# Sixteen-wide attentions: q and k in two float32r parts, two heads in the two row halves of the array, all masks on TensorE

## What is computed

```python
# L0_attn_a
q = (x @ Wq.T).reshape(b, s, 16, 16); k, v likewise
scores = einsum('bqhd,bkhd->bhqk', q, k) / sqrt(16)
scores = where(causal, scores, min)
out = einsum('bhqk,bkhd->bqhd', softmax(scores), v).reshape(b, s, 256)
y = out @ Wo.T
# L0_ffn: gate_pre = h @ W_in.T + 0.1 * tanh(attention(x) @ A) * (h @ A) @ B
# L3_attn_a: the same attention with biases on q, k, v and the output
```

## Time and profile before

| | us |
|---|---|
| median of 3 runs | 2940.77 (2939.55 to 2943.56) |
| the profiled execution | 2940.94, of it span 2939.2 |
| PE busy | 2789.6 (95%), 16121 matmul records |
| DVE busy | 1611.8 (55%) |
| ACT busy | 1325.1 (45%) |
| POOL busy | 613.7 (21%) |

### The profile page before, as it was taken

The page is one execution under the profiler, slowest core; times in us unless marked ns, Lnnn a source line. Parts: engine busy times, 40 slices in busy tenths (PEclk is TensorE's granted clock), DMA queues, the critical chain, the costliest instruction groups (busy, mean ns, idle before and its releaser), DMA issues. The chain is left out here.

```text
span 2939.2 us, 44166 instructions
## 1 busy us (share of the span) xinstructions
PE 2789.6 (95%) x16121; PEld 1865.1 (63%) x16121; DVE 1611.8 (55%) x3495; ACT 1325.1 (45%) x2711; POOL 613.7 (21%) x737
## 2 busy tenths in 40 slices
PE   7989998999999998999999999999999999989979
PEld 4454475644676886887666666676676767754545
DVE  7758545677446766764333333454333332478587
ACT  3745634546443333334433433444343433336576
POOL 2021002030012331432000000023333331130185
PEclk9999999999999999999999999999999999999989
DMA  3021010030103421531000000010000000121031
GB/s 99 22 62 55 3 50 28 1 85 6 53 12 90 126 82 39 151 111 50 11 17 11 12 11 24 1 34 17 11 17 11 17 35 13 40 55 35 13 98 55
DMA packets 69377, 122.17 MB, mean 42 GB/s; under 512 B 15790, under 2 KB 44816, under 8 KB 68896
## 3 DMA queue, kind: packets, MB, share of 16 engines
q1 hardware_dynamic: 67564, 118.04, 13.5%
q10 hardware_dynamic: 1600, 1.31, 0.3%
HBM read 92.21 MB, written 1.54 MB: 32 GB/s over the span
## 5 line engine op out<-in xcount | busy, mean ns | idle before, releaser
L236 POOL TENSOR_TENSOR scale<-scale,powers 128x1 f32<-128x1 f32 (+1 forms) x98 | 57.4, 586 | 1370.4 <-DVE scale L217 1370.4
L130 PE MATMUL psum<-L1f_hT_part,L1f_wide 128*128 128x512 f32 x1104 | 270.8, 395 | 8.4 <-DVE L1f_inner L2566 5.9
L130 PEld LDWEIGHTS psum<-L1f_hT_part,L1f_wide 128*128 128x128 f32 x1104 | 202.6, 189 | 53.0 <-DVE L1f_inner L2566 10.4
L1702 ACT ACTIVATE L2b_tanh<-psum,L2b_inverse 128x512 f32<-128x512 f32 x192 | 110.6, 579 | 269.7 <-PE psum L1650 268.3
L1281 ACT ACTIVATE L0f_weights<-psum 128x512 f32<-128x512 f32 (+2 forms) x320 | 157.0, 566 | 95.3 <-PE psum L1097 75.1
L2374 POOL TENSOR_TENSOR L1f_inner<-L1f_inner,L1f_weight 128x512 f32<-128x512 f32 x96 | 144.3, 1510 | 265.4 <-DVE L1f_inner L2566 179.7
L2139 ACT ACTIVATE L2a_probs<-psum,L2a_negmax 128x512 f32<-128x512 f32 (+7 forms) x128 | 95.0, 742 | 172.3 <-DVE L2a_negmax L2173 172.2
L1659 PEld LDWEIGHTS psum<-L2b_v,L2b_weights 128*128 128x128 f32 x1152 | 141.3, 193 | 40.2 <-issue 28.7
L130 PE MATMUL psum<-L1f_down,L1f_inner_part 128*128 128x256 f32 x1152 | 153.1, 284 | 8.3 <-DVE L1f_down L2577 4.2
L130 PEld LDWEIGHTS psum<-L1f_down,L1f_inner_part 128*128 128x128 f32 x1152 | 148.9, 191 | 15.6 <-DVE L1f_inner_part L2582 9.9
L2183 DVE COPY L2a_probsT<-psum 128x512 f32<-128x512 f32 (+1 forms) x64 | 31.4, 491 | 228.0 <-PE psum L2039 228.0
(11 more groups left out here) (555 smaller groups left out, 6267.4 us busy)
## 6 DMA issues: line engine op xcount, KB each, us to landing
L1f_w<-in_L1f_w SPq DMA_DIRECT2D x32, 384.0 KB, 3.5
L1f_weight<-combine SPq DMA_DIRECT2D x32, 384.0 KB, 4.3
L1f_weight<-combine SPq DMA_DIRECT2D x32, 256.0 KB, 4.8
scan_spread_b<-bc SPq DMA_DIRECT2D x16, 512.0 KB, 3.7
L0f_qs<-L0f_part SPq DMA_DIRECT2D x96, 64.0 KB, 2.6
experts_early<-in_L1f_w SPq DMA_DIRECT2D x16, 384.0 KB, 4.3
L2a_early<-in_L2a_w SPq DMA_DIRECT2D x16, 384.0 KB, 2.9
L2b_early<-in_L2b_w SPq DMA_DIRECT2D x16, 384.0 KB, 3.0
```

The lines of the kernel that those rows point to most:

```text
L130: last = nc.tensor.matmul(to, stationary, moving, start=start and n == 0, stop=stop and n == len(pairs) - 1, skip_group_check=skip)
L1702: nc.scalar.activation(tanhs[u % 3][:, at:], ps_scores[u % 3][:, at:], ACT.Tanh, scale=inverse[e][:, NT + kt:NT + kt + 1]).then_inc(capped, 1)
```

## The change

`TERMS` falls to three products and the parts are float32r, two of them: the first part is written as float32r by ACT for all eight projections, the second is what is left, by one DVE instruction for each (POOL has none of it any more). A stack has 48 rows, with the two parts of the maximum 50. The four heads of a quad lie in pairs: heads 0 and 1 in partitions 0 to 49, heads 2 and 3 in partitions 64 to 113, so `quad_columns` orders the weights' columns anew. A matmul over rows 0 to 47 (or 49) is followed at once by one over rows 64 to 111 (or 113), into another PSUM bank. Pieces come in pairs (`two_pieces`), and a score slot is one pair of heads. The custom DVE instruction and `core.late` are gone: all pieces on the diagonal get their mask on PE, over 128 rows, right behind their pair. Piece 0 of a half is now two pieces of two heads. Each stack of a quad and half still takes 12 DMAs, of 32 partitions of float32 where there were 64 of bfloat16; the rows of the maximum take two DMAs where there was one, and so do the ones.

```diff
-TERMS = [(0, 0), (0, 1), (1, 0), (1, 1), (0, 2), (2, 0)]
+TERMS = [(0, 0), (0, 1), (1, 0)]
 SPLIT = HD * len(TERMS)
-WITH_MAX = SPLIT + 3
-STACKED = 16 * 2 * len(TERMS)
+WITH_MAX = SPLIT + 2
+STACKED = 16 * 2 * 2 * len(TERMS)
+BY_HALF = (0, 2, 1, 3)
...
-    own = ([(0, half, 0, 4, P)] + [(1, half, j, 2, 2 * P) for j in (0, 2)]
-           + [(i, half, j, 1, (i + 1) * P) for i in (2, 3) for j in range(4)])
-    return [(i, 0, j, 1, HALF) for i in range(4) for j in range(4)] + own if half else own
+    own = ([(i, half, j, 2, (i + 1) * P) for i in (0, 1) for j in (0, 2)]
+           + [(i, half, j, 1, (i + 1) * P) for i in (2, 3) for j in BY_HALF])
+    return [(i, 0, j, 1, HALF) for i in range(4) for j in BY_HALF] + own if half else own
...
-        qs, ks = (st.sb(n, [WITH_MAX, 2, HEADS, HALF], BF16) for n in ("qs", "ks"))
+        qs, ks = (st.sb(n, [P, 2, QUADS, 2, HALF]) for n in ("qs", "ks"))
...
+        def stack_rows(j, count):
+            return slice(j // 2 * 64, j // 2 * 64 + count)
...
             for s, term in enumerate(TERMS):
-                if term[side] == part:
-                    engine.dma_start((qs, ks)[side][s * HD:(s + 1) * HD, half, 4 * q:4 * q + 4, :],
-                                     parts[n][part][q % 2 * 64:q % 2 * 64 + 64, half, :]
+                for e in range(2 if term[side] == part else 0):
+                    engine.dma_start((qs, ks)[side][e * 64 + s * HD:e * 64 + (s + 1) * HD, half, q, :, :],
+                                     parts[n, part, half][q % 2 * 64 + e * 32:q % 2 * 64 + e * 32 + 32, :].bitcast(F32)
...
-                to = own_bank(f"m{n}")
-                masks = kh == half and heads > 1
+                to = [own_bank(f"m{m}") for m in (n, n + 1)]
+                masks = kh == half
                 for e in range(heads):
...
+                    for part in range(2):
+                        j = PIECES[n + part][3] + e
+                        rows_of = stack_rows(j, SPLIT)
+                        last = nc.tensor.matmul(to[part][:, e * width:(e + 1) * width],
+                                                qs[rows_of, half, q, j % 2, i * P:(i + 1) * P].bitcast(F32R),
+                                                ks[rows_of, kh, q, j % 2, 0:width].bitcast(F32R), start=True, stop=not masks)
...
+                    for part in range(2 if masks else 0):
+                        b = (e + 1) * width
+                        last = nc.tensor.matmul(to[part][:, b - P:b], core.ident_bf[:], core.causal[:],
                                                 start=False, stop=True)
...
+                if mine[0] == 0:
+                    pe.wait_ge(firsts, len(PROJECTIONS))
+                    pe.wait_ge(seconds, len(PROJECTIONS))
+                    pe.wait_ge(ones_in, 32)
+                if mine[1] >= BANKS:
+                    pe.wait_ge(exped, mine[1] - BANKS + 1)
...
+                for i in range(heads):
+                    for n in mine:
...
+                        last = nc.tensor.matmul(head_part(n, i),
+                                                ks[rows_of, kt // 4, q, j % 2, kt % 4 * P:(kt % 4 + 1) * P].bitcast(F32R),
+                                                qs[rows_of, half, q, j % 2, at:].bitcast(F32R), start=True, stop=not masks)
...
+                    for n in mine if masks else ():
+                        last = nc.tensor.matmul(head_part(n, i)[:, 0:P], core.ident_bf[:], core.causal_turned[:],
                                                 start=False, stop=True)
...
-                if own and heads == 1:
...
-                    nc.vector.tensor_tensor_reduce(out=late_scores[n % 3][:, 0:width], in0=src,
-                                                   in1=core.late[:, HALF - width:], scale=1.0, scalar=-3.0e38,
-                                                   op0=ALU.add, op1=ALU.max, accum_out=to).then_inc(ring_free, 1)
-                else:
-                    nc.vector.tensor_reduce(to, src.rearrange("p (e k) -> p e k", e=heads), AX, ALU.max
-                                            ).then_inc(ring_free, 1)
+                nc.vector.tensor_reduce(to, src.rearrange("p (e k) -> p e k", e=heads), AX, ALU.max
+                                        ).then_inc(ring_free, 1)
```

More of the change, by code:

```diff
@@ L1080, in score @@
                 at = first_query(k)
[L1081 to L1097 removed]
+                mine = exps_of(slot)
```

255 lines of the change are left out of this document (101 added, 154 removed).

## The result

| | us |
|---|---|
| after, median of 4 runs | 3195.54 (3188.22 to 3201.79) |
| before, median of 4 runs beside it | 2941.05 (2939.55 to 2943.56) |
| after / before | 1.0863, 95% interval 1.0837 to 1.089 |
| the profiled execution after | 3198.72, of it span 3197.0 |

The sign was right and the size was not: +42 us forecast, +254 us measured. The page shows where to look. First the engines after, which answer to the earlier trace rows, and the slices of the granted clock, tenths of full speed in forty equal parts of the span; then the same slices before.

What follows compares the result with a forecast made beforehand. PE was taken to bound the later two thirds of a stage. PE's +12.2 us, less 2.2 hidden and 1.2 of DVE, plus 1 of waits and 0.6 at the start, gave 10.4 a stage, +42 over four: 2983 us, range 2950 to 3010.

Steps and rivals of the forecast that it cites:

- The pairs: Piece and score products: two matmuls in different row halves run side by side, -29.5 us a stage.
- Float32r: Paired products: 512 columns take 0.228 us where bfloat16 takes 0.216, +1.2 us a stage.
- Narrow float32r: Rival: float32r products of 128 columns cost up to 0.22 us, 5 us a stage, 3003 us; chance 0.12.
- The masks: Diagonal pieces of one head add 64 mask matmuls on PE at 0.058 us, +3.7 us a stage.
- The changes of shape: Around masked pairs: 309 switches of array shape instead of 62, 0.09 us of PE each, +22.2 us a stage.
- alternation is cheap: Rival: small row-half groups between full matmuls neither empty the array nor expose loads, 2909 us; chance 0.08.
- The weights: First pair after a shape change: its load lies open 0.10 us, 146 times, +14.6 us a stage.
- The waits: PE waiting for two free ring or score banks at once: 1 us a stage, between 0 and 4.
- PE idle for ACT in the slots without masks: Listed among the observations in the changed profile that would show the forecast wrong; no size given.
- The clock: In the 16-wide attention stretches the granted clock was read as 1.00, the 2.4 GHz level.
- PE's priced work: PE's sum of pairs, float32r, masks, shape changes and open weight loads: +12.2 us a stage.
- what I took as hidden: In the first 16 score slots, where DVE leads, 2.2 us more of PE a stage was counted as hidden.

Runs made afterwards that it cites:

- e1: The changed kernel with both products of a pair over all array rows, zeros between the stacks, instead of one row half each; 3121.03 us.
- e10: The kernel before with the one-head diagonal pieces also masked on PE and plain maxima on DVE; 2948.47 us.
- e2: The changed kernel with stacks, parts and maxima in bfloat16 instead of float32r; 3048.03 us.
- e17: The kernel before, with TensorE waiting for both score banks to be free before a two-bank slot's first product; 2959.85 us.
- e15: The changed kernel with every product over all 64 rows of its half, the added rows zero; 3188.90 us.
- e4: The changed kernel with each mask as two 64-row matmuls in the pair's own row halves; 3069.00 us.
- e5: The changed kernel with each of the 64 unmasked pairs of a stage run twice; 3145.20 us.
- e13: The kernel before without its masks on TensorE, stacks of 96 rows as before; 2924.07 us.
- e14: The kernel before without its masks on TensorE, with five products of parts and stacks of 80 rows; 2936.93 us.
- e9: The kernel before without its masks on TensorE, with three products of parts and stacks of 48 rows; 3020.01 us.
- e3: The changed kernel with all its masks left out; 3051.16 us.
- e16: The changed kernel in bfloat16 with masks in row halves, and every product over 64 rows, the added ones zero; 3003.25 us.
- e11: The changed kernel in bfloat16 with masks in row halves, and each unmasked pair run twice; 3013.20 us.

## Why the prediction was right in sign and wrong in size

**The pairs** held: the two of a pair start 0.003 us apart, and stream side by side. **Float32r** at 0.23 us for 512 columns held in row halves for a pair behind a pair; over all rows it didn't (e1, 0.33). **Narrow float32r** is not slow: a first pair of 128 columns is 0.26 us ahead of its mask, 0.10 + 0.06 + 0.09 and a rest of 0.01. That rival is out. **The masks** held (e10). **The changes of shape**, the term that the diff hides, held at 0.09, both ways, in small groups too, so the rival "alternation is cheap" is out. **The weights** held in size: the mask came 0.31 to 0.32 us after a first pair of 256 columns, where I had 0.30. They did not hold in their reason: with all 309 changes e2 has next to none of it (0.27 us to the mask, of which 0.16 are stream and 0.09 the change), so it comes with float32r, and the change of shape only stood beside it in the earlier trace rows. That the load is open because its 0.19 us outlast the masks in front is a guess. The prediction sets a rule of the Trainium skill, TensorE: Matmul & The Clock Gate, LDWEIGHTS, beside these 0.10 us, columns over 1.2 GHz, 107 ns for 128. That reading was wrong: the record of the float32r load is 0.19 us long, and a record of 0.10 belongs to the bfloat16 loads of e2, which cost next to nothing.

**The waits** failed. I let ACT's 0.49 us cover a pair and its way through the array "if PE comes at once", and took 1 us, up to 4, for the times when it doesn't. e17 measures 5 for the scores alone, and PE is idle for 9.3 us more a stage. The prediction named a sign of its being wrong, PE idle for ACT in the slots without masks, and it is there:

```profile
136.75 0.50 PE L1085 MATMUL psum<-L0a_qs,L0a_ks 50*128 50x512 f32 x2 [0.68 <-ACT L0a_weights L1268]
```

**The clock** is the step of the prediction that failed most. The prediction read "the granted clock is 1.00" from the rows of before and priced every term at that level, as if the clock were a property of the stage. It has no term, no rival and no chance in it. The clock changed with what the array does. The change halved the products' work (two times 48 rows side by side, where 96 rows streamed for twice as long), and put emptying, open loads and waits between them; half of the time in the stages was then at 1.2 GHz. Four single edits each gave back a part of the 473 us of half-clock time: filling the rows with zeros 134 (e15), masks in row halves 222 (e4), bfloat16 223 (e2), more columns 241 (e5). Rows by themselves move the clock (e13, e14, e9), and they are not all of it. Whether two halves of 48 rows side by side count as 96 rows no run tells.

How much is it? The stretches have 407 - 21 = 386 us more half-clock time. If all of it were a doubled stream on the path, each would be worth 0.5: 193 us, the most. e15 gives 0.39 for each, 150 us, and the masked group at both levels 0.38. Of the 247.8 us this leaves 55 to 98, 14 to 24 a stage, against the 10.4 of the prediction. As an estimate, PE's priced work (+12.2) and the idle time as measured (+9.3) make 21.5 a stage, near the upper end. So without the clock the forecast would still have been low, by a quarter to more than half, for the waits and for what I took as hidden. I can't split it further: e5 gives 0.45 for a microsecond, and the terms work on each other, since a lower clock lengthens the loads and the emptying and hides some of the waits.

One of my own tests for the prediction points the same way. PE should have been busy for over 97% of 80 to 160 us; it was for 76.37 of 80, 95%, with the clock at 0.69. The busy share hardly tells the difference.

The Trainium skill, TensorEngine Tiling (Array Packing), PSUM Pressure, says that row tiles must write to different PSUM banks; no run here tries it otherwise. The same page's PSUM Bottleneck says that after a faster TensorE the copies out of PSUM may become the bottleneck. The trace agrees: in L0a of e3 PE waits 14.0 us for ACT and 13.3 for DVE to read banks. The Trainium skill, TensorE: Matmul & The Clock Gate, Part 1, says that the clock is set by "how busy the PE has been recently". Here the measurement differs, if busy is read as the profile counts it: PE is busy for 20.00 of 20 us at 1.2 GHz in e9.

## What to carry to other kernels

When a change takes work off the array, give the clock a rival and a price of its own: it can fall while the busy share stays at 94%, and a microsecond at 1.2 GHz cost 0.38 to 0.45 us here. Two heads in the two row halves paid in none of these runs. What brought the kernel nearer was masks in row halves (127 us by themselves) and bfloat16 stacks (147), together still 1.6% behind the kernel before. Price a wait for two buffers by the run that has only this wait; a rule that looks covered by 0.49 us of another engine cost 5 us a stage.

## What the runs showed of the hardware that I had not expected

- The granted clock was 0.50 over 20 us in which PE was never idle (e9), and over the whole of L0a it went with the number of rows: 0.98, 0.93 and 0.80 for 96, 80 and 48 rows at the same columns (e13, e14, e9). Rows of zeros brought some of it back (e15, 0.75 to 0.81; e16, 0.92 to 0.96).
- More work made the kernel faster, by 50 us for 59 us of it (e5), where half of the time in the stages was at the low clock; in e11, where little of it was, it made the kernel 26 us slower.
- The first float32r pair behind masks of 128 columns costs 0.10 us more than in bfloat16, while its load's record is 0.19 us; behind a pair of 512 in row halves it costs nothing more. Over 112 and 114 rows products of 512 columns come every 0.33 us (e1), and over 128 rows in L1f every 0.228. Why is open.
